# Gelu in one pass over the first MLP half, and a planner with other offsets, in a two-layer AdaLN kernel

## The reference

```
# block 0, attention: windowed ("light") attention over the whole item, plus "heavy" attention
xn = layernorm(x)*(1+scale)+shift
light = softmax(q k^T / 8, window of 64 tokens to each side) v @ light_out_w     # 8 heads of 64
idx, score = top 256 of coordinate_descent(xn @ route_token)                     # 20 iterations
heavy = attention(q from 256 routed rows, k and v from 256 routed rows)          # written to rows idx
x = x + gate*(light + heavy)
# block 0, MLP: 64 small networks 1 -> 16 -> 1 with relu
# block 1, attention: causal, 16 heads of 16, q and k normalised per head and rotated
# block 1, MLP: 256 -> 1024 -> 256, weights binarised (alpha*sign(w))
x = x + gate*( gelu(xn @ w1.T + b1) @ w2.T + b2 )
```

## Time and profile before

| | |
|---|---|
| Median of three runs | 4390.54 us |
| The profiled execution's own time | 4394.76 us |
| Its span, first to last instruction | 4393.0 us |
| TensorE (PE) busy | 3662.8 us, 83% |
| DVE / ACT / POOL busy | 2511.7 / 1934.2 / 1486.2 us (57 / 44 / 34%) |
| Mean granted TensorE clock | 0.90 of full |
| One item in the steady part | about 507 us |

### The profile page before, as it was taken

How to read it: one execution, slowest core, us unless ns; L and a number is a source line. 1 busy time by engine, 2 the same in 40 slices (tenths; PEclk the granted TensorE clock), 3 DMA queues, 4 the chain that set the end, 5 groups by cost and what they waited for, 6 DMA issues and landing times. The chain is left out here.

```text
span 4393.0 us, 59749 instructions
## 1 busy us (share of the span) xinstructions
PE 3662.8 (83%) x19241; PEld 2053.7 (47%) x19241; DVE 2511.7 (57%) x6732; ACT 1934.2 (44%) x4521; POOL 1486.2 (34%) x1807
## 2 busy tenths in 40 slices
PE   6378569987799878997799887998799887998787
PEld 2245334464446534464445544465344654465433
DVE  6754547357563666547573665636574565736652
ACT  5134334544264443554355442644435443544433
POOL 4133342244323441234412433234412444134311
PEclk8589789998899988998899988998899988999788
DMA  6110231002300022002300023002210023000120
GB/s 229 67 32 13 48 77 31 14 15 48 93 13 23 24 60 69 18 12 50 88 20 13 22 44 90 15 22 44 67 45 14 12 52 93 13 24 22 42 58 6
DMA packets 207650, 191.30 MB, mean 44 GB/s; under 512 B 12993, under 2 KB 189377, under 8 KB 207306
## 3 DMA queue, kind: packets, MB, share of 16 engines
q1 hardware_dynamic: 203298, 177.94, 16.0%
q0 software_dynamic: 3328, 8.39, 0.7%
q10 hardware_dynamic: 720, 1.15, 0.1%
HBM read 121.73 MB, written 65.11 MB: 43 GB/s over the span
## 5 line engine op out<-in xcount | busy, mean ns | idle before, releaser
L2322 ACT ACTIVATE arena<-pb 128x512 f32<-128x512 f32 (+3 forms) x1536 | 670.9, 491 | 338.9 <-PE pb L1557 333.1
L2402 POOL TENSOR_TENSOR arena<-arena,small 128x512 f32<-128x512 f32 x256 | 284.7, 1116 | 481.8 <-DVE small L1732 481.4
L2151 ACT ACTIVATE arena<-arena,small 128x256 f32<-128x256 f32 x512 | 256.0, 500 | 416.9 <-DVE small L1715 416.3
L2566 POOL TENSOR_SCALAR_AFFINE_SELECT arena<-arena 128x256 f32<-128x256 f32 x512 | 219.5, 432 | 603.0 <-ACT arena L2322 601.7
L1574 PE MATMUL pb<-arena,v 128*17 128x512 f32 (+3 forms) x3072 | 368.1, 512 | 28.4 <-POOL arena L2566 19.7
L2006 DVE TENSOR_REDUCE arena<-pb 128x1 f32<-128x512 f32 x512 | 333.1, 682 | 97.6 <-PE pb L1532 96.4
L1557 PE MATMUL pb<-arena 98*128 98x512 bf16 (+3 forms) x1152 | 355.0, 344 | 11.3 <-ACT arena L2322 6.6
L1715 DVE CUSTOM_DVE_ANT_0 arena<-pb,wmask 128x256 f32<-128x256 f32 x512 | 196.0, 420 | 237.8 <-PE pb L1274 237.8
L1998 DVE TENSOR_REDUCE arena<-pb 128x4 f32<-128x512 f32 x256 | 173.0, 688 | 232.1 <-PE pb L1523 229.9
L1274 PE MATMUL pb<-arena 128*128 128x256 f32 x1024 | 285.8, 405 | 5.2 <-issue 4.5
L1652 PE MATMUL pb<-xh,w1T 128*128 128x512 f32 x512 | 267.0, 662 | 10.0 <-DVE xh L1872 8.6
(11 more groups left out here) (354 smaller groups left out, 7597.4 us busy)
## 6 DMA issues: line engine op xcount, KB each, us to landing
split_q<-arena SPq DMA_DIRECT2D x384, 64.0 KB
arena<-split_q SPq DMA_DIRECT2D x64, 384.0 KB, 5.4
split_k<-arena SPq DMA_DIRECT2D x192, 64.0 KB
arena<-split_k SPq DMA_DIRECT2D x24, 384.0 KB, 6.4
xn<-h_d SPq DMA_DIRECT2D x8, 1024.0 KB, 11.7
xt<-in_x SPq DMA_DIRECT2D x16, 512.0 KB, 3.9
heavy_d<-arena SPq DMA_DIRECT2D x8, 1024.0 KB, 4.4
xn<-heavy_d SPq DMA_DIRECT2D x8, 1024.0 KB, 5.5
```

What stands on the lines that cost most here:

```text
L2151: ins = s.activation(pm[n % 3][:, j], sm[n % 2][:, j], ACT.Exp, bias=nmx[:, 2 * sl + j:2 * sl + j + 1], scale=-1.0, accum_out=sml[:, 2 * s ...
L2322: s.activation(pp[pn % 4][:, h % 2, 0:w_], bank[n % 3][:, 0:w_], ACT.Exp).then_inc(a_exp1, 1)
L2402: g.tensor_tensor(pm[n % 3], pm[n % 3], rcl[:, 2 * sl:2 * sl + 2].unsqueeze(2).broadcast_to([P, 2, 2 * P]), ALU.mult).then_inc(p_norm0, 1)
L2566: g.affine_select(out=p2, in_=p2, pattern=[[0, 2], [1, P]], compare_op=ALU.is_ge, fill=0.0, base=0, channel_multiplier=-1).then_inc(p_tri, 1)
```

## The change

**Gelu.** In `mlp1(b, 0)` the 8 tiles leave PSUM with Identity (bias added), and then a single Gelu runs over all of `g1` in place, 128 x 4096 elements; the first `w2T` product waits for it (semaphore `a_gel`). `mlp1(b, 0)` gets one step more. In `mlp1(b, 1)` the 8 Gelus stay, but the first `w2T` product waits for all of them at once. The row statistics of `mlp1` wait for the last addition of the attention output instead of one tile each.

**Planner.** `LAG` 14 to 8; `HNORM_BEHIND_ATT` 46 to 31; `HEAVY_BEHIND_ATT` 15 to 10; the opening fills of `att(b, 1)` 40 to 42 (`AHEAD`), and the last of the other fills at score step 20 instead of 21. Two gates that let the first step of `mlp1(b, 0)` begin two steps before the end of `att(b, 0)` are gone.

**First setup block.** All 48 column products are made at item u = 3 instead of a third each at 3, 4 and 5; ACT copies the scores of item u-1 after it has taken both turned halves of item u, not between; DVE's variance comes after the two turned halves.

```diff
-    ("att", 0): 12 + 6 + 1 + 16 + 2 + 6, ("att", 1): 28 + 12 + 1 + 32 + 2 + 6,
-    "hrows": 16, "heavy": 58, "chain": 42, ("mlp1", 0): 24, ("mlp1", 1): 24, "hnorm": 10,
+    ("att", 0): 12 + 6 + 1 + 16 + 2 + 6, ("att", 1): 28 + 14 + 1 + 32 + 2 + 6,
+    "hrows": 16, "heavy": 58, "chain": 42, ("mlp1", 0): 25, ("mlp1", 1): 24, "hnorm": 10,
-HROWS_BEHIND_MLP, HEAVY_BEHIND_HROWS, HEAVY_BEHIND_ATT, HNORM_BEHIND_ATT, ... = 10, 12, 15, 46, 11, 1
+HROWS_BEHIND_MLP, HEAVY_BEHIND_HROWS, HEAVY_BEHIND_ATT, HNORM_BEHIND_ATT, ... = 10, 12, 10, 31, 11, 1
-LAG = 14
+LAG = 8
-        gate["mlp1", b, 0] = [(("att", b, 0), steps_of(("att", b, 0)) - 2), (("chain", b, 3), 42)]
+        gate["mlp1", b, 0] = [(("att", b, 0), steps_of(("att", b, 0))), (("chain", b, 3), 42)]
-AHEAD = (6, 12)
-LAST_FILLS = ((1, 5, 9), (4, 12, 21))
+AHEAD = (6, 14)
+LAST_FILLS = ((1, 5, 9), (4, 12, 20))
@@ setup, vector
                         statistics(u + 2)
-                        variance(u + 2)
                     take_turned(2 * u)
                     take_turned(2 * u + 1)
+                    if u + 2 < B:
+                        variance(u + 2)
@@ setup, scalar
-                        if u and h == 0:
-                            take_scores(u - 1)
                         take_turned(2 * u + h)
+                    if u:
+                        take_scores(u - 1)
@@ setup, tensor
+                        columns_of(MODC)
                         t.wait_ge(v_set, mark["row0"])
-                    if 3 <= u:
-                        if u > 3:
-                            t.wait_ge(a_rows, u - 3)
+                        rows_of(1)
+                    elif 4 <= u < 8:
+                        t.wait_ge(a_rows, u - 3)
                         rows_of(u - 2)
-                    if 3 <= u < 6:
-                        columns_of(MODC[2 * (u - 3):2 * (u - 2)], 2 * (u - 3))
@@ mlp1, tensor
+                    if c == 0:
+                        yield
+                        t.wait_ge(a_gel, b + 1)
+                    else:
+                        t.wait_ge(a_g, FT * (H + 1))
                     for i in range(TH):
...
                         for k in range(FT):
-                            if i == 0:
-                                t.wait_ge(a_g, FT * H + k + 1)
                             mm = t.matmul(...)
@@ norm_half, vector
+                    v.wait_ge(p_o1, TH * (H + 1))
                     for i in range(TH):
-                        v.wait_ge(p_o1, TH * H + i + 1)
@@ mlp1, scalar
-                        gelu_tables[0] = True
-                        s.activation(g1[:, m], bank[banks[m % len(banks)]], ACT.Gelu,
-                                     bias=cols[:, C_FB1 + m:C_FB1 + m + 1]).then_inc(a_g, 1)
+                        gelu_tables[0] = gelu_tables[0] or c == 1
+                        s.activation(g1[:, m], bank[banks[m % len(banks)]], ACT.Identity if c == 0 else ACT.Gelu,
+                                     bias=cols[:, C_FB1 + m:C_FB1 + m + 1]).then_inc(a_g, 1)
+                        yield
+                    if c == 0:
+                        s.wait_ge(a_g, FT * (H + 1))
+                        gelu_tables[0] = True
+                        s.activation(g1, g1, ACT.Gelu).then_inc(a_gel, 1)
                         yield
```

More of the change, by code:

```diff
@@ L79 @@
     "begin": 1, "start": 1, ("light", 0): 17 + 2 * (UNITS + 6), ("light", 1): 12 + 2 * (UNITS + 6),
-    ("att", 0): 12 + 6 + 1 + 16 + 2 + 6, ("att", 1): 28 + 12 + 1 + 32 + 2 + 6,
-    "hrows": 16, "heavy": 58, "chain": 42, ("mlp1", 0): 24, ("mlp1", 1): 24, "hnorm": 10,
+    ("att", 0): 12 + 6 + 1 + 16 + 2 + 6, ("att", 1): 28 + 14 + 1 + 32 + 2 + 6,
+    "hrows": 16, "heavy": 58, "chain": 42, ("mlp1", 0): 25, ("mlp1", 1): 24, "hnorm": 10,
 }
-PACE = {('light', 0): (1.88, 0.9), ('light', 1): (1.0, 1.0), ('att', 0): (1.79, 0.9, 0.9), ('att', 1): (1.0, 1.28, 0.8)}
+PACE = {("light", 0): (1.88, 0.9), ("light", 1): (1.0, 1.0), ("att", 0): (1.79, 0.9, 0.9), ("att", 1): (1.0, 1.28, 0.8)}
 CHAIN_AHEAD = (12, 2)
-HROWS_BEHIND_MLP, HEAVY_BEHIND_HROWS, HEAVY_BEHIND_ATT, HNORM_BEHIND_ATT, ATT_BEHIND_MLP, MLP_BEHIND_LIGHT = 10, 12, 15, 46, 11, 1
+HROWS_BEHIND_MLP, HEAVY_BEHIND_HROWS, HEAVY_BEHIND_ATT, HNORM_BEHIND_ATT, ATT_BEHIND_MLP, MLP_BEHIND_LIGHT = 10, 12, 10, 31, 11, 1
 LOAD_STEP = 8
-LAG = 14
+LAG = 8
 def steps_of(key):
@@ L144, in turn @@
         if key[0] == "chain" and key[2] == 3 and n == 41 and not reached([(("chain", key[1], 2), 42), (("att", key[1], 0), 22)]):
-            return
-        if key[0] == "mlp1" and key[2] == 0 and n == 1 and not reached([(("att", key[1], 0), steps_of(("att", key[1], 0)))]):
             return
@@ L496, in _ @@
                         count(v.tensor_copy(cmask[:, :], cmf))
-                    if u == 6:
-                        v.wait_ge(t_mod, 4)
+                    if u == 4:
+                        v.wait_ge(t_mod, 2)
                         count(v.tensor_copy(modc[:, :, :].rearrange("p j b -> p (j b)"), bank[6][:, 0:6 * KD * B]))
@@ L565, in rows_of, with columns_of @@
                     mm.then_inc(t_rows, 1)
-                def columns_of(parts, first=0):
-                    for j, (blk, part) in enumerate(parts, first):
+                def columns_of(parts):
+                    for j, (blk, part) in enumerate(parts):
                         for kk in range(KD):
@@ L1117, in adaln_kernel @@
         row_in = [sem(f"row_in{j}") for j in range(2)]
-        t_w1, a_g, t_w2, v_w2, p_w2 = (sem(n) for n in ("t_w1", "a_g", "t_w2", "v_w2", "p_w2"))
+        t_w1, a_g, a_gel, t_w2, v_w2, p_w2 = (sem(n) for n in ("t_w1", "a_g", "a_gel", "t_w2", "v_w2", "p_w2"))
         view = zone(arena, 0)
@@ L2085, in mlp1 @@
                     yield from norm_half(b, c, banks)
-                    for _ in range(FT):
+                    for _ in range(FT + (c == 0)):
                         yield
```

## The result

The changed kernel took 4512.27 us (median of 4 runs, 4509.07 to 4525.22), the kernel before beside it 4392.39 us (4390.48 to 4394.76): 1.0276 times as long, 95% interval 1.0261 to 1.0292, some 120 us more. Forecast were 4477 us, 87 us more, in a range up to 4512. The direction and most of the size were right; 33 us are missing, and the time lies at the upper end of the range, just outside.

What follows compares the result with a forecast made beforehand. The prediction took PE, busy 83% of the span, as the bound of the whole. Its terms summed to 86.8 us on the profiled 4394.8 us, giving 4481.6 us in profile and 4477 us as median, range 4438 to 4512 us.

Steps and rivals of the forecast that it cites:

- Gelu in one pass, and the clock behind it: In each item's `mlp1(b, 0)`: uncovered table load and Gelu cost 5.5 us, lower PE clock 2.5 us; 44 + 20 us.
- hnorm earlier: `hnorm` moves among the opening fills of `att(b, 1)`, its DVE work partly delaying PE: 1.5 us an item, 10.5 us.
- two more opening fills: Before the score steps: two turns of 1.6 us more, partly given back in the score steps; net 1 us an item, 8 us.
- first setup block: Once: later scores' copy delays dots 2.7 us for items 6 and 7, moved columns give some back; 4.5 us (-1 to 8).
- LAG: First two chains, once: shorter tail -13 us, against DVE waiting 4 us and chain steps 4 us; -5 us (-13 to 2).
- `mlp1(b, 1)`, statistics: First `w2T` product waits one Gelu longer, 7 times: 4 us; statistics behind all four additions at the last `mlp1`: 0.8 us.
- DVE as the bound by hnorm: Rival, opening fills of `att(b, 1)`: all 6.2 us of `hnorm` hit PE, 33 us more, 4510 us; chance 0.12.
- Cheap clock: Rival, `w2T` products: the clock doesn't fall behind the Gelu pause, or costs little; 20 us less, 4457 us; chance 0.10.
- A drain of 1.38 us at each switch: Rival, ACT table switch in `mlp1(b, 0)`: unhidden switch takes 2.66 us, 8 x 1.38 us more, 4488 us; chance 0.03.
- The swallowing stretch: Rival: 11.0 us of idle PE time an item before the score steps absorbs the delays, 4395 us; chance 0.05.

Runs made afterwards that it cites:

- Gelu alone: Kernel before with only the `mlp1(b, 0)` change: Identities, table load, one Gelu, one planner step more, two gates gone; 1.0149 of before, 65 us longer.
- hnorm alone: Kernel before with `hnorm` moved behind step 31 of `att(b, 1)` instead of 46, its lag 8, and the new `HEAVY_BEHIND_ATT`; 1.0029 of before, 13 us longer.
- fills alone: Kernel before with 14 opening fills of the second group instead of 12, last fills by score step 20 instead of 21; 1.0033 of before, 14.5 us longer.
- LAG alone: Kernel before with a lag of 8 turns instead of 14 for the first two chains only; 1.0013 of before, 6 us longer.
- variance alone: Kernel before with only DVE's variance moved behind the two turned halves in the first setup block; 1.0032 of before, 14 us longer.
- variance back: Changed kernel with DVE's variance again in front of the turned halves in the first setup block; 1.0254 of before, 10 us less than the changed kernel.
- `shift` behind `offset`: Changed kernel with POOL's `shift` of item u waiting for DVE's `offset` of item u+2; 1.0256 of before, 9 us less than the changed kernel.
- the scores' run: Kernel before with only ACT's copy of the scores moved behind both turned halves in the first setup block; 1.0025 of before, 11 us longer.

## Why the prediction was too low

Its own steps, in us of the whole run (in brackets the interval, where runs give one):

| step | forecast | measured | by |
|---|---|---|---|
| Gelu in one pass, and the clock behind it | 44 + 20 | 65 (59 to 72) | Gelu alone |
| hnorm earlier | 10.5 | 13 (7.5 to 18) | hnorm alone |
| two more opening fills | 8 | 14.5 (9 to 20) | fills alone |
| first setup block | 4.5 | 25.3 | traces |
| LAG | -5 | 6 (1 to 11) | LAG alone |
| `mlp1(b, 1)`, statistics | 4.8 | 0.1 (-12 to 13) | what is left |
| sum | 86.8 | 120 (115 to 128) | |

*The step that failed is the first setup block*, "4.5 us (-1 to 8)": 20.8 us, where the misses of all steps add up to 37 and the whole was missed by 33. It was mis-sized twice. The variance was not priced at all: the prediction's term has no word on it. What moved with its small instructions is the moment at which `power` and then `offset` start, and in the new place each of them meets a long instruction of the other engine: `offset` takes 4.48 us for 0.15, in six of eight turns. That lock is shown by four runs (variance alone, variance back, `shift` behind `offset`, and the scores' run, where it is absent). And the scores' copy was priced at 2.7 us in two turns; alone, in the turns of items 5 and 6, it cost 3.4 and 4.0, since 1.7 us of lower clock came with the pause there, and the turns up to item 4, which I took to be free, lost 4.6 us: 12.1 us. A third miss is that the parts were added up as if they were independent: the columns were free only as long as DVE stood for a load.

*LAG* had the wrong sign. Six chain steps that go beside other work were taken at 4 us, against 13 us of tail; the light half beside them took 14 us more.

*Gelu and its clock* held, wait and clock apart: 8 x 5.84 = 47 us for 44, and 8 x 1.67 = 13 us in the products behind it for 20; the rest of the 65 lies inside the scatter. The lower clock is worth about 1.5 us here (5.13 for 3.62 us), and not the 1.8 and 2.2 us of the earlier trace rows.

*hnorm and the fills* were right in kind, in front of the score steps, and low by 2 and 6.5 us: the fills give back 1.45 us behind the score steps but nothing in them.

*`mlp1(b, 1)` and the statistics* weren't tried alone; the parts measured alone leave 0.1 us for them, with an uncertainty of some 12 us, which tells little. The trace shows the mechanism of the prediction: the first `w2T` product of `mlp1(3, 1)` waits 1.14 us where the earlier trace rows have 0.56, and three Gelus stand in the last group for two.

```profile
2461.26 3.72 PE L1666 MATMUL pb<-w2T,arena 128*128 128x256 f32 x16 [1.14 <-ACT arena L2366]
```

From the first `w1T` to the first `w2T` product it is 0.6 us more in three of seven items, 7.1 us in item 5 (not explained), 1.5 us on the mean; with the products behind it, and 0.34 us given back in front of it, the traces have 13 us in seven items for the 4 of the sum.

*The rivals.* DVE as the bound by hnorm: no, 13 us and not 43. Cheap clock: no, though nearer than thought. A drain of 1.38 us at each switch, the rule of the Trainium skill, "ScalarE: Activation LUTs", section "What ACT_TABLE_LOAD costs": the trace shows load and next activation back to back (2232.50 + 1.28 = 2233.78, Gelu at 2233.79), and hiding the load gives 1.31 us, not 2.66. The swallowing stretch: no, 42.10 us after the Gelu's delay.

*The sums.* One does not come out: sum without the clock's cost, `LAG` at its best, and `mlp1(b, 1)`, the setup block and the statistics at nothing give 4440 us for the lower end, not 4438.

*What stays open.* The two runs that take 21.4 and 17.8 us out of the setup block were 9 and 10 us shorter than the changed kernel in time, at most 19 by the intervals. The run without the setup part of the change was 23 us shorter (14 to 32), which fits the 25.3. In the traces of the four kernels with the changed items these take 88 us (`shift` behind `offset`), 92 (changed kernel), 94 (without its setup block) and 103 us (variance back) more than before, though their order is the same. I take the difference for such scatter; whether the items give some of it back isn't settled.

## What to carry to other kernels

Before moving a small instruction, look who else starts at the new place: some DVE and POOL operations on SBUF that begin within each other's length run one after the other (here those with two inputs and a small one with one, but not the statistics), and the small one pays the long one's length. A group whose mean is several times the usual time of such an instruction is that sign, and can be read before anything is changed. Edits that share a loop don't add up: one can use up the wait that hid another. An edit that costs one engine a little in a loop has to be priced by what sets that loop in each turn, with the clock behind the new pause.

## What the runs showed of the hardware

A DVE operation of 128x8 with two inputs in SBUF took 0.15 to 0.17 us free and 4.46 to 4.51 us behind a POOL add of 128x2048; a POOL power of 128x8 took 1.65 us free and 3.62 us when it began 0.17 us behind the start of a DVE multiply of 128x2048 (2.29 us); begun 1.28 us ahead of one it took 1.65 us. An operation with one input, all in SBUF, was held too: `L441`, at 45.01 us before, took 1.24 us instead of 0.17 and ended at 46.25 us, with POOL's `shift` (41.68 + 4.54 = 46.22):

```profile
45.01 1.24 DVE L441 TENSOR_SCALAR small<-small 128x8 f32<-128x8 f32 x1
```
```profile
41.68 4.54 POOL L627 TENSOR_TENSOR arena<-arena,w1T 128x2048 f32<-128x2048 f32 x1 [1.99 <-DVE arena L460]
```

The statistics weren't held: eight of them ran in 2.70 us from 49.88 us on, all beside the `shift` of 49.96 us. A Gelu of 128x4096 from SBUF took 3.62 us, eight of 128x512 from PSUM 0.69 us each. And of the twelve PE pauses of 2.75 us in front of the dots, in the three runs that have them (the scores' run, `shift` behind `offset`, variance back), five were followed by dots of 5.29 us, at the lower clock in part, and seven by dots of 3.59 us.
